# Attention scores on 32 rows a head: plain and shifted scores alternate on two row groups of TensorE

## The reference, cut to what matters

```python
q, k, v = proj(layernorm(x), Wq, bq), proj(ctx, Wk, bk), proj(ctx, Wv, bv)   # 16 heads, HD = 8
scores = jnp.einsum('bhqd,bhkd->bhqk', q, k) / math.sqrt(HD)
scores = jnp.where(mask[:, None, None, :] == 0, -1e10, scores)
p_attn = jax.nn.softmax(scores, axis=-1)
a = jnp.einsum('bhqk,bhkd->bhqd', p_attn, v).transpose(0, 2, 1, 3).reshape(nb, seq, H * HD) @ Wo + bo
x = x + jnp.tanh(g_xattn[0]) * a
x = x + jnp.tanh(g_ffn[0]) * ffn(layernorm(x))     # experts: not touched
```

## Time and profile before

| | |
|---|---|
| three runs | 465.22, 465.64, 468.93 us; median 465.64 us |
| span of the profiled execution, first to last instruction | 464.5 us (the time measured around this execution is not among the three; the span lies 1.1 us under their median) |
| busy: PE, DVE, ACT, POOL | 392.2, 387.9, 341.6, 316.3 us |
| attention | from about 38 us (first score) to about 229 us |

### The profile page before, as it was taken

How to read it: one execution, slowest core, us unless ns; L and a number is a source line. 1 busy time by engine, 2 the same in 40 slices (tenths; PEclk the granted TensorE clock), 3 DMA queues, 4 the chain that set the end, 5 groups by cost and what they waited for, 6 DMA issues and landing times.

```text
span 464.5 us, 13551 instructions
## 1 busy us (share of the span) xinstructions
PE 392.2 (84%) x4611; PEld 297.0 (64%) x4611; DVE 387.9 (84%) x951; ACT 341.6 (74%) x674; POOL 316.3 (68%) x439
## 2 busy tenths in 40 slices
PE   0457998997999899987789897999999999999910
PEld 0335777785887787765534343444699999999910
DVE  7596678978777977799696799777799999999986
ACT  0635687787888788877668657888688888888854
POOL 6242222799899999978777777775067777777750
PEclk9999999999999999999899899999999999999975
DMA  7978884354444253555001111111313333355229
GB/s 190 285 209 222 187 182 107 89 135 95 107 101 105 61 119 92 148 213 185 26 6 53 51 53 46 46 51 55 80 60 93 101 90 97 90 147 171 73 67 295
DMA packets 71825, 53.22 MB, mean 115 GB/s; under 512 B 7481, under 2 KB 63620, under 8 KB 71760
## 3 DMA queue, kind: packets, MB, share of 16 engines
q1 hardware_dynamic: 64752, 43.02, 34.9%
q0 software_dynamic: 4544, 8.44, 5.5%
q10 hardware_dynamic: 2464, 0.91, 0.8%
HBM read 29.38 MB, written 24.33 MB: 116 GB/s over the span
## 4 chain that ended last, share of the span: by engine, by line
PE 46%; DVE 22%; POOL 12%; issue 5%; DMA 5%; ACT 4%; SPq 2%; DVEq 0%; POOLq 0%; ACTq 0%
PE pAtt L1143 11%; PE pAtt L1080 6%; PE pS L1131 5%; PE pE L1131 5%; PE pS L1018 3%; DVE HH L1508 3%; PE pE L1018 3%; DVE t_MX L1257 3%; DMA scr<-QKS 2%; PE pS L880 2%; PE pMix L1121 2%; POOL t_STG L541 2%; POOL t_W2l L545 2%; POOL QKS L531 2%; PE pAtt L919 1%
## 5 line engine op out<-in xcount | busy, mean ns | idle before, releaser
L637 POOL DMA_INDIRECT yd<-Y,XR x78 | 86.8, 1113 | 40.6 <-issue 23.2
L1257 DVE TENSOR_REDUCE t_MX<-pS 128x4 f32<-128x512 f32 x128 | 86.9, 682 | 22.7 <-PE pS L880 20.2
L735 ACT ACTIVATE PT<-pE,t_mbias,t_scl 128x512 f32<-128x512 f32 x128 | 97.0, 789 | 2.9 <-PE pE L880 2.7
L611 POOL DMA_INDIRECT xs<-t_STG,t_pos x64 | 65.6, 1024 | 21.5 <-issue 14.8
L1536 DVE SCALAR_TENSOR_TENSOR HR<-G,t_sc,HR 128x512 f16<-128x512 f32 x78 | 58.6, 751 | 2.8
L1143 PE MATMUL pAtt<-t_W2h,HR 128*128 x624 | 59.2, 219 | 0.8 <-DVE HR L1536 0.7
L880 PE MATMUL pS<-t_K,t_Q 128*128 128x128 f16 x512 | 52.5, 229 | 7.8 <-DVE t_MX L1257 5.1
L1508 DVE SCALAR_TENSOR_TENSOR HH<-H,t_sc,HH 128x512 f16<-128x512 f32 x64 | 48.2, 764 | 8.2 <-ACT HH L789 6.3
L1143 PE MATMUL pAtt<-t_W2l,HR 128*128 x312 | 54.4, 219 | 0.0
L820 ACT ACTIVATE G<-pS,t_b1T,t_inv 128x256 f32<-128x256 f32 x78 | 40.0, 563 | 17.1 <-PE pS L1131 16.1
L880 PE MATMUL pE<-t_Q,t_K 128*128 128x128 f16 x512 | 50.2, 221 | 1.9 <-DMA t_Q<-MPl 1.0
(11 more groups left out here) (276 smaller groups left out, 1008.6 us busy)
## 6 DMA issues: line engine op xcount, KB each, us to landing
xs<-t_padrow SPq DMA_DIRECT2D x10, 516.0 KB, 5.0
XR<-xs SPq DMA_DIRECT2D x39, 129.0 KB, 2.3
scr<-QKS SPq DMA_DIRECT2D x16, 256.0 KB, 2.4
t_Q<-scr SPq DMA_DIRECT2D x16, 256.0 KB
t_K<-scr SPq DMA_DIRECT2D x32, 128.0 KB
t_STG<-in_W SPq DMA_DIRECT2D x7, 512.0 KB, 6.8
YY<-yd SPq DMA_DIRECT2D x14, 256.0 KB, 4.9
t_X<-in_x SPq DMA_DIRECT2D x4, 512.0 KB, 6.1
```

Of the source, the lines that this page charges most:

```text
L611: g.indirect_dma_start(k.xs, bass.IndirectOffsetOnAxis(ap=pos[:, n:n + 1], axis=0), k.PAY[:, n, :], None).then_inc(h.di[q], 16)
L637: g.indirect_dma_start(k.yd, bass.IndirectOffsetOnAxis(ap=XR[u][:, q, D:ROW], axis=0), Y[u][:, q, :], None, bounds_check=2 * T - 1, oob_is ...
L735: act.activation(PT[:, m % NPT], pE[g % 2][:], ACT.Exp, bias=k.mbias[:, bt:bt + 1], scale=k.scl[:, bt:bt + 1]).then_inc(s.exp, 1)
L1257: v.tensor_reduce(out=MX[:, n // G % 2, n % G // 4, m % 2, m // 2::2], in_=pS[n % 2][:], axis=AX_X, op=ALU.max).then_inc(s.max, 1)
```

## The change

A head still has 32 rows, but four heads now lie in four groups of 32 rows of both `Q` and `K`, with four column blocks of such fours. No rows are kept at zero. The mask slot of a head has eight rows, of which the mask now takes four, two hold zeros, and the two others (rows 27 and 31 of the head) are the shift rows: zero in `Q` as it is loaded from the scratch, and overwritten by the shift DMAs. The DMA that copied zero rows and the clearing of `Q` and `K` go away; the keys come in one DMA and not two; the mask is half as many rows; more constant rows are written to the scratch once at the start. A score matmul takes the 32 rows of its head, so that step g runs on row group g modulo 4. PE issues shifted and plain scores alternately. They are of different steps and so lie on two different row groups and in two banks.

```diff
-SLOT_ROWS = 4 * HD
-SHIFT = 2 * SLOT_ROWS
+ROWS = 4
+HEAD_ROWS = P // ROWS
+MASKED = 4
+SHIFT = 4 * HD - 5
...
             for u in range(NB):
-                sp.dma_start(k.scr[u][0, :, 3, :], k.constq[:]).then_inc(k.s_pad, 16)
+                sp.dma_start(fourth(u, 0)[:, 0:MASKED, :], k.constq[:]).then_inc(k.s_pad, 16)
+                sp.dma_start(fourth(u, 0)[:, MASKED:HD, :], k.nothing[:]).then_inc(k.s_pad, 16)
+                sp.dma_start(fourth(u, 1)[:, MASKED:HD, :], k.constk[:]).then_inc(k.s_pad, 16)
             sp.wait_ge(k.s_one, 16)
             key_mask(0)
-            for u in range(NB):
-                if u == NB - 1:
-                    sp.wait_ge(s.zk, 1)
-                for par in range(2):
-                    sp.dma_start(k.K[u][SHIFT + 2 * par:SHIFT + 2 * par + 2, par::2, :], k.constk[:]).then_inc(k.s_padk, 16)
...
                     wait(sp, s.ST, G * (t - NB + 1))
-                    sp.dma_start(k.Q[u][SHIFT:SHIFT + 4, :, :], k.Q[u][SHIFT + 4:SHIFT + 8, :, :]).then_inc(s.rd[u], 16)
...
-                    sp.dma_start(k.Q[u][0:SHIFT, :, :], scr[0].rearrange("(h2 pd) s t -> (pd s) h2 t", pd=2 * HD)).then_inc(s.rd[u], 16)
-                    for par in range(2):
-                        src = scr[1].rearrange("(h2 par d) s t -> par (d s) h2 t", par=2, d=HD)[par]
-                        sp.dma_start(k.K[u][SLOT_ROWS * par:SLOT_ROWS * (par + 1), par::2, :], src).then_inc(s.rd[u], 16)
+                    for op, into in ((0, k.Q[u]), (1, k.K[u])):
+                        sp.dma_start(into[:], scr[op].rearrange("(j rd) s t -> (rd s) j t", rd=ROWS * HD)).then_inc(s.rd[u], 16)
...
+            def score(n, j, out, transposed):
+                g, u = n % G, n // G % NB
+                rows, q = slice(HEAD_ROWS * (g % ROWS), HEAD_ROWS * (g % ROWS + 1)), S * (g // 4)
+                qo, ko = k.Q[u][rows, j, q:q + S], k.K[u][rows, j, q:q + S]
+                return pe.matmul(out[:, j, :], ko if transposed else qo, qo if transposed else ko, start=True, stop=True)
+
+            def scores(n, m):
+                plain, less = 0 <= n < G * NP, 0 <= m < G * NP
+                if less:
+                    if m % G == 0:
+                        pe.wait_ge(s.m[m // G % NB], N_M * (m // G // NB) + N_M)
+                    wait(pe, s.exp, m - 1)
+                if plain:
+                    if n % G == 0:
+                        pe.wait_ge(s.rd[n // G % NB], N_RD * (n // G // NB) + N_RD)
+                    wait(pe, s.max, n - 1)
+                for j in range(4):
+                    if less:
+                        to = score(m, j, pE[m % 2], True)
+                    if plain:
+                        of = score(n, j, pS[n % 2], False)
+                if less:
+                    to.then_inc(s.ST, 1)
+                if plain:
+                    of.then_inc(s.S, 1)
...
-                    less(m + 1)
-                    plain(G * (t - 1) + g - PH + 1)
+                    scores(G * (t - 1) + g - PH + 1, m + 1)
```

More of the change, by code:

```diff
@@ L142, in _ @@
                 g.memset(k.constq[:], MASK16)
-                g.memset(k.constk[:], BIG16)
-                clear_keys(g, k, 0).then_inc(s.init, 1)
+                g.memset(k.nothing[:], 0.0)
+                g.memset(k.constk[:], BIG16).then_inc(s.init, 1)
                 g.wait_ge(s.init, 1)
@@ L151, in _ @@
                 g.affine_select(out=k.lower[:], in_=k.lower[:], compare_op=ALU.is_gt, fill=0.0, base=0,
[L152 to L155, removed]
+                                pattern=[[1, P]], channel_multiplier=-1).then_inc(s.init, 1)
                 g.wait_ge(s.init, 2)
@@ L257, in layer @@
     PT = bg("PT", [P, NPT, 4, S])
-    in_pair = lambda t: t[0:2 * HD].rearrange("p (a b) -> p a b", a=2)
-    MPT = [[in_pair(hi), bg(f"MPl{u}", [2 * HD, 2, S], F16)[:]] for u, hi in enumerate((k.constk, k.constq))]
+    in_pair = lambda t: t[0:H].rearrange("p (a b) -> p a b", a=2)
+    MPT = [[in_pair(hi), bg(f"MPl{u}", [H, 2, S], F16)[:]] for u, hi in enumerate((k.constk, k.constq))]
     bvr = bg("bvr", [P, P])
@@ L874, in _ @@
             pe.matmul(bias_cols, bvr[:], k.Wo[:], start=True, stop=True).then_inc(s.any, 1)
-            def scores(g, u, out, transposed):
-                for j in range(4):
-                    hd, q = head(g, j), S * (g // 4)
-                    qo, ko = k.Q[u][:, hd // 2, q:q + S], k.K[u][:, hd, q:q + S]
-                    ins = pe.matmul(out[:, j, :], ko if transposed else qo, qo if transposed else ko, start=True, stop=True)
-                return ins
-            def plain(n):
-                if not 0 <= n < G * NP:
-                    return
-                pair, g = n // G, n % G
-                if n == 0:
-                    pe.wait_ge(k.s_padk, 32 * NB)
-                if g == 0:
-                    pe.wait_ge(s.rd[pair % NB], N_RD * (pair // NB) + N_RD)
-                wait(pe, s.max, n - 1)
-                scores(g, pair % NB, pS[n % 2], False).then_inc(s.S, 1)
@@ L895, in less @@
-            def less(m):
-                if not 0 <= m < G * NP:
-                    return
-                pair, g = m // G, m % G
-                if g == 0:
-                    pe.wait_ge(s.m[pair % NB], N_M * (pair // NB) + N_M)
-                wait(pe, s.exp, m - 1)
-                scores(g, pair % NB, pE[m % 2], True).then_inc(s.ST, 1)
+            def score(n, j, out, transposed):
[3 more added lines that the diff above has]
+                return pe.matmul(out[:, j, :], ko if transposed else qo, qo if transposed else ko, start=True, stop=True)
@@ L1256, in maximum @@
                     wait(v, s.nmT, n // G - 1)
[L1257 removed]
+                v.tensor_reduce(out=MX[:, n // G % 2, n % G // 4, m, :], in_=pS[n % 2][:], axis=AX_X, op=ALU.max).then_inc(s.max, 1)
             def less_maxima(t):
@@ L1599, in program @@
         k.s_c, k.s_x = ([outer.enter_context(nc.semaphore(f"{n}{c}")) for c in range(NT // CHUNK)] for n in ("c_ctx", "c_x"))
-        k.s_one, k.s_pad, k.s_padk, k.s_b2, k.s_rest = (outer.enter_context(nc.semaphore("c_" + n)) for n in ("one", "pad", "padk", "b2", "rest"))
+        k.s_one, k.s_pad, k.s_b2, k.s_rest = (outer.enter_context(nc.semaphore("c_" + n)) for n in ("one", "pad", "b2", "rest"))
         k.keep = outer
-        alloc(outer, k, MX=([P, 2, 2, 2, HD], F32), PV=([P, 2, 2, S], F32),
+        alloc(outer, k, MX=([P, 2, 2, ROWS, 4], F32), PV=([P, 2, 2, S], F32),
               REC=([P, 2, H], F32), AK=([P, 2, H, HD], F32), AT=([P, 2, S], F32), ST6=([P, 2, 6], F32), XF=([P, 2, D], F32),
```

40 lines of the change are left out of this document (18 added, 22 removed).

## The result

The changed kernel takes **476.98 us** (median of 4 runs, 475.06 to 477.89) against 465.88 us before: a ratio of 1.0246, 95% interval 1.0192 to 1.03. I had forecast 464.8 with a range of 460.5 to 472.5. The kernel is slower by 11 us, beyond the range.

What follows compares the result with a forecast made beforehand. POOL's splitting was taken to bound the attention from 83 to 201 us, SP's queue before it and DVE after; the terms summed to -0.8 on the 464.5 us span, 463.7, forecast as 464.8 us against the median, range 460.5 to 472.5.

Steps and rivals of the forecast that it cites:

- The overlap: Score matmuls of a step: eight on two row groups take 0.22 us, not 0.44, saving 1.76 us a turn.
- The switch: Between 32-row scores and whole-array work: 0.23 us a visit, five more visits, 1.15 us a turn.
- PE is in order: Waits ahead of a step's first score: PE runs in order, so only 0.22 us of pE matmuls a step move.
- the waits: All waits of a step now stand before its first score, for both kinds of score; counted as nothing.
- Term (a): 38 to 51 us, only plain scores: about five new switches on the path, 0.12 each or more, +0.6 us.
- PE's turn: Middle of the attention: PE's own work goes from 10.2 to 9.6 us a turn, with 0.8 us of waiting besides.
- POOL's pace from 117 to 201: Term (e): POOL's splitting sets the pace there, with turns of 10.98 us, so the change brings nothing.
- The DMAs: Term (b), SP's queue up to the keys at 76.11: one key DMA for two, -0.9 us, bounds 0 and 2.
- The keys at turn 5: PE's wait for the keys at 76.11 us should be less than the 1.04 us of before.
- the clock: Rival: gaps from paired scores and switches delay the clock's rise by a turn or two; 471 us (468 to 476), chance 0.10.
- far outside my range: Clock falling in the middle of the attention: each turn at the lower level would cost 8 us.
- term (f): 201 to 229 us: DVE sets the pace, the gain is carried, three or four new switches on the path, +0.4 us.

Runs made afterwards that it cites:

- the run in sequence: Changed kernel, with the four shifted scores of a step first and the four plain ones behind them, not alternating; 484.96 us, 1.0378 of the kernel before.
- the run with all rows: Changed kernel with every score matmul on all 128 rows, so each sums four heads; 462.54 us, 0.9949 of the kernel before.
- The run with added switches: Kernel before, with a small extra 32-row matmul in five of a turn's eight steps, so ten more switches; 471.02 us, 1.0147 of before.
- the grouped early run: Changed kernel, scores of the first four pairs on all 128 rows, fours grouped by tiling in mixed steps; 471.05 us, 1.0118 of before.
- early copies: Changed kernel, with spare 128-row float32 matmuls in PE's waits from 15 to 48 us; 474.03 us, 1.019 of the kernel before.
- late grouped: Changed kernel, scores of the last four pairs on all 128 rows, fours grouped by tiling in mixed steps; median 473.49 us, ratio 1.011.
- The second stretch of the pieces: Separate kernel of TensorE alone, without waits (364.2 us whole): its stretch of 32-row matmuls on one group, 57 us at granted clock 0.50.
- the mixed steps: Changed kernel, steps with one score kind on 32 rows, the other on 128: alternating 492.57 us (late), 490.67 (early); grouped 473.49 and 471.05.

## Why the prediction was wrong, step by step

*The overlap* (0.22 us for eight) was right: 0.056 us from pair to pair. *The switch* (0.115 each, a visit 0.23) was right: about 0.10 each, a visit 0.21 to 0.24. *PE is in order* was not: matmuls on another row group start ahead of earlier ones, as the run in sequence shows; the waits, which I had counted as nothing on that ground, cost nothing all the same in the run with all rows. *Term (a)*, five switches at the lower clock for +0.6, fits: counted from the first split, the fourth comes at 27.1 us instead of 26.4. *PE's turn* (9.6 of work and 0.8 of waiting) was right: where PE leads the chain at full clock, behind 130 us, ACT's copies for the projections come at 130.15, 140.35 and 150.56, a turn of 10.2. *POOL's pace from 117 to 201* was right where the clock was up: 10.97 a turn from 134 to 189. *The DMAs* (-0.9, between 0 and -2) could not come true here. SP does issue two loads instead of three, and what follows is shorter,

```profile
58.88 0.45 SPq L466 DMA_DIRECT2D t_Q<-scr  x1
59.37 0.51 SPq L466 DMA_DIRECT2D t_K<-scr  x1
...
61.12 1.66 SPq L413 DMA_DIRECT2D kwm<-t_tops  x1
```

(1.11 for the two key loads alone and 2.81 for the store before). But the split comes so late under the half-clock PE that SP waits for it (65.65 us to the next scratch write, 64.13 before). The kernel with all rows, faster than before by 0.9 to 3.9 us, has the sign of the term, but its earlier rise of the clock enters there too, so no run sizes it. *The keys at turn 5*: PE no longer waits for DMA there, but a half-clock PE arrives late, so this confirms little.

**The step that failed is the clock.** The sum took the granted clock of the kernel before, and the clock stood among the rivals with a chance of 0.10 and 471 us, as a later rise by a turn or two; the 477 measured lies beyond even the 468 to 476 given to it. I reasoned that paired scores and switches leave gaps. The run with added switches shows that ten more a turn don't do it, and the stretch of 57 us on one row group that no gap is needed. A later rise alone, by the grouped early run, costs 2.5 to 4 us, which I had priced at 6.5. What I put "far outside my range", a fall in the middle, came twice. Its price was mis-sized as well: I wrote 8 us for each turn at the lower level; 14 us at 112 to 126 cost 1.9, and 34 us at 204 to 238 cost 6, since PE had waited for DVE there at full clock. So term (f), "201 to 229: DVE's pace, +0.4", is the one with the largest error: PE at half clock is the bound of that stretch, +7.2 against the kernel before.

What is shown: with its scores on 32 rows this kernel loses its clock, and the lost time follows the clock. From 199 to 250 us the runs with 32-row scores and no copies there were at half clock for 20 to 34 us, and those with 128-row scores for 3 to 10. The time from the last split to the first down matmul goes along: 57.0 us with 34 us at half clock (the changed kernel; 56.9 in the run in sequence), 56.2 with 31 (early copies), 53.1 with 20 (early grouped), 51.3 with 10 (all rows), 50.9 and 49.8 with 3 (late grouped; the kernel before). The run with added switches, 52.2 with 3, lies above the row by their own cost. The run with all rows excludes layout, DMAs and coupled waits, and the run with added switches excludes ten switches a turn by themselves.

What is not shown is by what property 32-row scores lose the clock in the kernel. Its runs don't part fewer rows from the shorter time of overlapped scores, nor from switches together with few rows. From 211 us on only shifted scores are left and nothing overlaps, and the changed kernel stays at half clock there; but it came in at half clock, and the late grouped run did not. The second stretch of the pieces shows that few rows can do it alone, and the mixed steps suggest that many switches count as well.

What also stays open is how rows, breaks and the column tiles of the values add up. Steps with 32-row scores kept the clock when TensorE ran alone, while the kernel, at 207 to 233 us, didn't regain it with PE busy for 26.00 of 26 us. Nor did I find a correct version that beats both kernels: the run with the new layout that is about 2 us faster has its scores on the whole array, where it can't compute one head at a time.

## What to carry to other kernels

Packing small contractions on row groups halves their time, but each whole-array piece between them costs two switches (0.2 us here, all that four pairs save), so group by tiling before packing. A tighter matmul can slow everything behind it through the clock: before the edit, look at which engine sets the pace in each stretch and ask what a TensorE at half clock would do there. A run of the same kernel on all rows shows what the tiling costs as a whole, its switches and its clock together. Tilings shouldn't alternate within a step.

## What the runs showed of the hardware

- TensorE on 32 rows of one group, busy for 57.00 of 57 us, stayed at the lower level (0.50); on two groups in turn it kept 1.00.
- Matmuls on another row group overtake: pS was issued behind four pE and started 0.01 to 0.02 us behind the first.
- The moment at which the clock rises differs between executions of the same instructions: 39, 50 and 52 us with 128-row scores, 64, 77 and 80 us with 32-row scores.
- With score matmuls that alternate between 32 and 128 rows (seven switches among eight) the clock was at half for 24 us (188 to 213); with the same ones grouped by tiling it kept 1.00 from 172 to 233 us.
- A change between 32-row and whole-array tiles costs 0.10 us in either direction (0.16 us from matmul to matmul when alternating, 0.056 without a change).
